# Eight scatters of a batch: four groups of two in place of two groups of four

## The reference

```
x = x + attention(layernorm(x))      # 16 heads of 16, band |i-j| <= half,
                                     # softmax, W_o per head, then Wfc
x = x + ffn(layernorm(x))            # 8 experts, the best 2 of each token:
    gating = softmax(X @ Wg + bg);  top 2
    expert = (silu((X@W1+b1) * (X@W3+b3))) @ W2 + b2
    mixed  = sum(weight * expert) @ Wf + bf
```

## Time and profile before

| | |
|---|---|
| median of 3 runs | 1354.57 us |
| the profiled execution, device time | 1353.25 us |
| its span | 1351.5 us |
| PE busy | 1175.3 us (87%) |
| DVE busy | 970.8 us (72%) |
| ACT busy | 782.4 us (58%) |
| POOL busy | 605.6 us (45%) |
| L744, the scatters of the attention part, x128 | 130.5 us, mean 1020 ns |
| L754, the low weight parts, x24 | 54.0 us, mean 2280 ns |

### The profile page before, as it was taken

How to read it: one execution, slowest core, us unless ns; L and a number is a source line. 1 busy time by engine, 2 the same in 40 slices (tenths; PEclk the granted TensorE clock), 3 DMA queues, 4 the chain that set the end, 5 groups by cost and what they waited for, 6 DMA issues and landing times. The chain is left out here.

```text
span 1351.5 us, 47132 instructions
## 1 busy us (share of the span) xinstructions
PE 1175.3 (87%) x18161; PEld 869.7 (64%) x18177; DVE 970.8 (72%) x2167; ACT 782.4 (58%) x1463; POOL 605.6 (45%) x648
## 2 busy tenths in 40 slices
PE   4798898888888889888888259999999999999996
PEld 2464555555555545555454148888888888888885
DVE  5345868789787877878766537777777777777775
ACT  4347776776767767677565125544555445455553
POOL 2301324546545465554535715444444444454454
PEclk9899999999999989999896679999999999999999
DMA  4875554766646666465725244656645755645554
GB/s 147 242 227 115 159 149 120 210 165 188 180 111 196 166 192 175 116 183 144 213 58 176 86 135 63 110 85 125 133 57 68 176 78 71 126 65 70 64 64 48
DMA packets 211580, 177.54 MB, mean 131 GB/s; under 512 B 115522, under 2 KB 175562, under 8 KB 211290
## 3 DMA queue, kind: packets, MB, share of 16 engines
q1 hardware_dynamic: 153482, 117.78, 34.0%
q0 software_dynamic: 25728, 34.17, 15.0%
q10 hardware_dynamic: 32208, 23.33, 6.6%
HBM read 67.99 MB, written 89.90 MB: 117 GB/s over the span
## 5 line engine op out<-in xcount | busy, mean ns | idle before, releaser
L1642 PE MATMUL p_h<-xt_parts,w_hi 128*128 128x256 f16 x1824 | 273.7, 273 | 7.3 <-DVE xt_parts L1729 6.9
L1058 DVE TENSOR_REDUCE mx<-p_max 128x4 f32<-128x496 f32 (+1 forms) x248 | 211.4, 853 | 93.2 <-PE p_max L1340 92.7
L855 ACT ACTIVATE probs<-p_exp,unscale 128x736 f32<-128x736 f32 (+1 forms) x256 | 210.3, 821 | 76.1 <-PE p_exp L1340 50.3
L1788 POOL DMA_INDIRECT out<-yw,tokens x136 | 220.7, 1623 | 45.9 <-POOL tick L1787 34.7
L1733 DVE SCALAR_TENSOR_TENSOR t<-p_h,b,t 128x256 f32<-128x256 f32 x272 | 125.8, 481 | 105.3 <-ACT t L1681 99.7
L1642 PEld LDWEIGHTS p_h<-xt_parts,w_hi 128*128 128x128 f16 x1824 | 177.4, 98 | 31.3 <-DVE t L1733 9.7
L1787 POOL TENSOR_TENSOR tick<-tick 128x1 f32<-128x1 f32 x136 | 65.4, 481 | 265.4 <-ACT yw L1698 265.4
L1681 ACT ACTIVATE t<-p_h,b,undo 128x256 f32<-128x256 f32 x272 | 142.1, 554 | 67.8 <-PE p_h L1642 62.9
L1642 PE MATMUL p_h<-xt_parts,w_lo 128*128 128x256 f16 x912 | 174.0, 273 | 0.0
L744 POOL DMA_INDIRECT routed<-rows,slots x128 | 130.5, 1020 | 38.9 <-issue 38.9
L1375 PE MATMUL p_out<-probs,v 64*32 64x184 f32 (+1 forms) x4096 | 138.1, 327 | 8.3 <-DVE out_t L1071 7.7
(11 more groups left out here) (274 smaller groups left out, 2524.3 us busy)
## 6 DMA issues: line engine op xcount, KB each, us to landing
qk_dram<-qk_hi SPq DMA_DIRECT2D x128, 128.0 KB, 2.6
qs<-qk_dram SPq DMA_DIRECT2D x64, 192.0 KB, 4.3
ks<-qk_dram SPq DMA_DIRECT2D x64, 192.0 KB, 4.3
x_in<-in_x SPq DMA_DIRECT2D x64, 128.0 KB, 3.4
qk_dram<-qk_lo SPq DMA_DIRECT2D x64, 128.0 KB, 2.4
w_mat<-in_W ACTq DMA_DIRECT2D x32, 256.0 KB
out<-x_sb SPq DMA_DIRECT2D x64, 128.0 KB
w_split<-w_first_hi SPq DMA_DIRECT2D x24, 256.0 KB
```

The source lines that it names most:

```text
L855: nc.scalar.activation(probs[r % 3][:, :, 0:hi - lo].rearrange("p (e s) w -> p e s w", e=2), p_exp[:, :, 0:2 * WIN].rearrange("p e (s w) - ...
L1058: nc.vector.tensor_reduce(out=maxes, in_=max_buffer(r, p_max, p_exp)[:, :, 0:2 * WIN].rearrange("p e (s w) -> p e s w", s=2)[:, :, :, 0:hi ...
L1642: last = nc.tensor.matmul(p_h[:, m % KC, k, :], w[e][a][:, k, HID * c + P * m:HID * c + P * m + P], xt[:, x, c, :], start=(n == 0 and c == ...
L1788: nc.gpsimd.indirect_dma_start(out=io["out"].rearrange("b s d -> (b s) d"), out_offset=bass.IndirectOffsetOnAxis(ap=tokens[:, b, :].bitcas ...
```

## The change

The eight scatters of a batch are issued in four groups of two, at entries 52, 57, 60 and 62 (rounds 4, 9, 12 and 14 of step b+3), in place of two groups of four at entries 52 and 61 (rounds 4 and 13). `scatter` takes a part 0 to 3: its upper bit picks the expert, its lower bit the half of the four token tiles. The batches from 13 on have two parts at each of their entries.

```diff
-SCATTER_AT = (52, 61)
-PROMPT_AT = (47, 52)
+SCATTER_AT = (52, 57, 60, 62)
+PROMPT_AT = (47, 47, 52, 52)
...
-            def scatter(b, j):
-
-                if j == 0:
+            def scatter(b, part):
+
+                j, half = part // 2, part % 2
+                if part == 0:
                     pool.wait_ge(s_placed, b + 1)
                     pool.wait_ge(s_lo2, b + 1)
                     pool.wait_ge(s_noted, b + 1)
-                for t in range(NT):
+                for t in range(2 * half, 2 * half + 2):
                     nc.gpsimd.indirect_dma_start(...)
```

## The result

| | before | changed |
|---|---|---|
| median of the runs | 1354.57 us | 1370.22 us (1367.46 to 1374.19, 3 runs) |
| the profiled execution, span | 1351.5 us | 1368.5 us |
| granted clock over the span | 0.960 | 0.951 |
| ratio, 95% interval | | 1.0118 [1.0096, 1.0140] |

Run again beside the kernel before, later on, the changed kernel took 1.0085 [1.0059, 1.0112] of its time. It is slower by about 1%, 14 to 16 us. One of those seven later runs took 1433.17 us at a granted clock of 0.84, a slower state of the chip, and is not part of the ratio.

The account below looks back on a forecast made before the run. Exponentials set the pace, held in odd steps by ACT's load waiting for POOL's third low part. 5.1 + 4.8 - 0.5 - 0.7 = +8.7 us on the median 1354.57, rounded down: 1363, range 1357 to 1371.

Parts of the forecast that it names:

- third low part: POOL, six odd steps: it ends later by 14.8 - 6.9 - 2.8 = 5.1 us in all; bounds 3 and 8.
- the clock: TensorE, odd steps: longer PE gaps bring a full drop to half level in two more steps, 4.8 us; bounds 0 and 9.6.
- the end: From step 15, POOL is the path: two more scatters against an earlier note, net -0.7 us; bounds -1.8 and +2.5.
- Round 9's pair: POOL: two scatters ahead of the last weight part delay ACT's load 2.47 us in each of six odd steps, 14.8 us.
- The low parts: POOL, odd steps: DVE's division meets a scatter instead and no longer collides, 6 x 0.47 = 2.8 us less.
- The drain: POOL's second_norm, odd steps: with two scatters outstanding it falls to 0.15 us, gaining 6.9 us; bounds nothing and 6.9.
- Even steps: Steps without weight work: keys should land earlier behind fewer scatters, 0.5 us gained over all; bounds -3 and +1.
- Round 14's pair: POOL, between note with split 0 and split 1: split 1 comes 2.5 us later, costing nothing.
- A: Rival: POOL's delays reach ACT but the clock does not fall oftener; +4 us, 1358.5; chance 0.24.
- B: Rival: faster, gains outrun the cost of the two scatters in round 9; -4.5 us, 1350; chance 0.09.
- C: Rival: off the path, DVE work already behind takes up the delay; +-1, 1354.5; chance 0.13.

Follow-up runs that it names:

- round-11 kernel: Changed kernel with the second two scatters moved from round 9 to round 11, behind POOL's third low part: 1345.45 us, 0.9936 of the kernel before.
- late-groups kernel: Changed kernel with the second two scatters back in round 4, so only the last four are split (rounds 12 and 14): 1354.99 us, 1.0002 of the kernel before.
- first experiment: Changed kernel with the last four scatters together again in round 13, leaving two in round 9: 1370.28 us, 1.0118 of the kernel before.
- second comparison: The changed kernel, unaltered, run again beside the kernel before on another chip: 1365.96 us, 1.0085; the kernel before took 1352.01 us.
- first group: First of three sets of experiment runs, each on a chip of its own; the kernel before had a median of 1354.55 us in it.

## Why the prediction was right, point by point

The path was the forecast's: pair, third low part, ACT's load, exponential, PE, clock. Slower was forecast at 1363.0, and 1370.22 lies 0.8 us inside the range's upper end. The three runs were 6.7 us apart, so that it lay inside is in part luck. Three terms were too small: the delay of the third low part, the clock and the end.

Of the signs named, most came: ACT's load 0.04 us behind the third low part, ACT idle for 3.84 to 4.61 us there, the clock down in all six odd steps, even steps of 39.53 to 39.98 us. Two did not: the drain was not 0.15 us, and the odd steps took 42.41 to 46.81 us, not 43 to 45.5.

- **Round 9's pair**, forecast 2.47 us a step, measured 2.74, 16.4 instead of 14.8 us. Its first scatter took 1.29 us, not 1.04. DVE's timeline of step 9 shows what it meets, and two lines of POOL in step 14 of the kernel before, where a division began 0.08 us ahead of the last scatter of four (696.59), show the same:

```profile
498.32 1.43 DVE L1080 TENSOR_TENSOR wf<-out_t,sums 128x512 f32<-128x512 f32 x1
```
```profile
695.41 0.96 POOL L744 DMA_INDIRECT routed<-rows,slots  x1 [0.30 <-issue]
696.67 1.44 POOL L744 DMA_INDIRECT routed<-rows,slots  x1 [0.30 <-issue]
```

The division stands until the second low part ends (499.21) and finishes under the scatter, 499.75. In the round-11 kernel it also took 1.43 us, and a low part behind it was the one lengthened: the three took 6.76 us together, against 6.35 us here.
- **The low parts**, forecast 2.8 us less in all, measured 0.4 a step, 2.4. But of these 0.25 us a step came back in the scatter. The Trainium skill ("SBUF — State Buffer", section "Who interferes with whom") infers that generating descriptors needs the write interface, while a two-input DVE instruction takes only the read interface. The trace agrees for the division, which finished during the scatter, but the scatter took 0.25 us longer beside it, which the inference does not provide for. The kernel before showed this already: beside a division of 0.69 us a scatter took 1.44 us in step 8 and in step 14, where the one ahead of it in step 14 took 0.96. The prediction looked only at the division. Why the scatter pays, no run here shows.
- **The drain**, forecast 0.15 us, measured 0.31 in four steps, 0.32 in step 3 and 0.47 in step 13: 5.7 us gained instead of 6.9. Two things set its length. With four scatters just ahead it ends with their landing, 3.25 to 4.81 us after POOL was done with the last one. In the changed kernel the pair is done at 490.31 and the drain begins at 494.53, 4.22 us on; its last packet had ended at 493.22. So two scatters fewer put the landing out of the drain. What is left is no wait for the landing, and it went by how many scatters were issued since the drain before: in `norm`, 12.2 us behind the pair of round 14, there is the same 0.31 us (POOL, step 9 of the changed kernel):

```profile
486.05 0.20 POOL L719 TENSOR_TENSOR shift<-less,rs 128x4 f32<-128x4 f32 x1 [0.31 <-issue]
```

With none issued since the last drain it was 0.14 to 0.15 us, with two 0.31 or 0.32, with four 0.47 (step 13 of the changed kernel, which has no `norm` in between) and with six 0.64 (step 14 of the late-groups kernel). The prediction took the length with none for a pair.
- **The third low part** was therefore later by 16.4 - 2.4 - 5.7 = 8.3 us, not 5.1; by step, from the variance on, 1.91, 1.63, 1.16, 0.70, 1.40 and 1.51. That is just above the bound of 8. The exponentials' gaps grew by 7.1 us, 2.0 more than forecast.
- **The clock** was the step that I trusted least, and it was mis-sized by 1.9 us, about as much as the gaps: two of four steps at 2.4 us were forecast, all four fell, at 1.36 to 2.29 us (7.5 us in all), less 0.9 us in steps 9 and 13: 6.7 instead of 4.8. The size of 2.4 us was somewhat high (1.9 on average), the count was wrong. None of this was measured with the clock held. All six gaps came out alike at 6.2 to 6.5 us, and in the kernel before one of 5.51 us had already had its drop; there was no reason to let two of them pass.
- **Even steps**, forecast -0.5, measured -0.3. **Round 14's pair** cost nothing, as the first experiment shows.
- **The end**, forecast -0.7, measured +0.9. Here the working was wrong. POOL in and after step 15:

```profile
747.36 0.21 POOL L732 COPY rows<-gates 128x32 f32<-128x32 f32 x1
752.07 0.39 POOL L734 TENSOR_SCALAR token<-token 128x4 f32<-128x4 f32 x1 [4.50 <-issue]
753.26 1.08 POOL L745 DMA_INDIRECT routed<-rows,slots  x1 [0.81 <-issue]
...
759.71 0.96 POOL L745 DMA_INDIRECT routed<-rows,slots  x1 [0.30 <-issue]
```

The note's second half starts at 752.07; before it did at 740.43. Step 15 started 13.2 us later, so it is 1.6 us sooner, not the 3.2 that I credited: the drain fell from 5.80 only to 4.50 us. It ends with the landing of the last scatter, issued last as ever: by the DMA records the last packet on the scatters' queue ended at 751.43 us, 0.64 us ahead of the drain's end, and at 739.63 us, 0.80 ahead, in the kernel before. POOL was done with that scatter 29.0 us into the step, against 29.3 before. Behind it stand six scatters in a row instead of four, 2.5 us more. 2.5 - 1.6 = +0.9. The prediction's bound of -1.8 us does not follow from the rows that it names either: from 755.24 to 757.60 there are 2.36 us.

Sum of the parts: 7.1 + 6.7 - 0.3 - 0.7 (step 14) + 0.9 + 0.4 (before step 3) = 14.1 us up to the expert part. The expert part's 2.9 us, taken as unchanged, are spread between executions, and so is what the medians' 15.65 us have over the 14.1; the second comparison gave 1365.96 - 1352.01 = 14.0 us.

The rivals: A (queue alone) falls with the rest column, as far as the rest is the clock's. B fell because no step's gain exceeded the pair; it would have come true with the pair two rounds later, where the same gains in the drain stand against no insertion. C falls: ACT's idle time grew by 13 us and the gaps with it.

## What to carry to other kernels

Before an instruction is put into an in-order queue, ask which waits hang on what stands behind it: two scatters two rounds later are 1.8% faster here, at the same count and in the same queue. Read an idle time named "issue" or named after an innocent engine together with the DMA issue that ends it, since a DMA's wait holds the engine's queue. And where several steps come to the same gap length, count on a fall of the clock in all of them; how long it lasts can still differ (3.4 to 10.2 us behind gaps of 6.1 to 6.5 us in the first experiment).

## What the runs showed of the hardware that I had not expected

- POOL's drain behind indirect DMAs: 0.14 us with none issued since the last drain, 0.31 us after a pair even when that was 12.2 us ago, 0.47 us after four that had landed, and in the odd steps up to 2.53 us shortly after four, when it ended 3.25 to 4.81 us behind the last one. Whether it carries the spread of the kernel before (1343.38 to 1361.12 us in 24 runs of the first group) is not shown: the round-11 kernel, whose drains in the odd steps are 0.31 to 0.47 us, spread over 11.1 us in nine runs too.
- TensorE at the half level behind idle times of 3.0 to 3.4 us in front of the held score (changed kernel); behind those of 0.86 to 0.90 us, in steps 3 to 11 of the round-11 kernel, the record stayed at 1.00.
- A group of runs, on a chip of its own, in which the same program took 8% longer, with 28 to 49 us of TensorE idle time that no view names. There the order of the kernels is another: a change of this size should be timed on more than one chip.
